# Two layer norms finished on ScalarE, two subtractions and additions moved into PSUM, and a new order of VectorE's work in a fused RWKV and FP4 kernel

## The chip, the cores and the metric

The kernel runs on one core of one Trainium2 chip. The metric is the device time of one execution in microseconds (us); lower is better. The engines are called by the profile's names: PE (TensorE, with PEld for its weight loads), DVE (VectorE), ACT (ScalarE), POOL (GpSimd) and SP (SyncE, which issues the DMAs). PSUM is the memory that PE writes; SBUF holds all else on the chip.

## What is computed

Input is x of 4 x 1024 x 256 in float32. A time-mixing block with a decaying state and a feed-forward block with block-wise quantised operands follow one another, each behind a residual and a layer norm.

```python
xx = jnp.concatenate([x[:, 1:2, :], x[:, :-1, :]], axis=1) - x
xk = x + xx * time_mix_k            # and xv, xr, xg
r = xr @ W_r.T; k = xk @ W_k.T; v = xv @ W_v.T
g = jax.nn.sigmoid(xg @ W_g.T)
state = state * w + k_t v_t^T ; out_t = state @ r_t      # scan over t, 16 heads of 16
y = attn * g @ W_o.T
y = (y - mu) / jnp.sqrt(var + EPS) * ln_gamma + ln_beta
x = _layernorm(x + y)
...
scale = jnp.max(jnp.abs(xb), axis=-1, keepdims=True) / 6.0      # blocks of 16
q = _GRID[jnp.searchsorted(_MID, jnp.abs(xb / scale))] * jnp.sign(xb) * scale
h = jax.nn.silu(q(x) @ q(w_gate).T) * (q(x) @ q(w_up).T)
x = _layernorm(x + q(h) @ q(w_down).T)
```

## The kernel before

The 4096 tokens are 32 tiles of 128 (NT = 32, 8 to a batch, TPB = 8). The work is a software pipeline: in step n every engine does its part of several tiles at once. Each engine has its own function `tiles()` whose loop runs n from 0 to 35, and the instructions of an engine run strictly in the order in which they stand there. Engines meet at semaphores (`wait_ge`, `then_inc`). Nothing but this order and the semaphores sets when something runs. A second path for fast decays exists, is chosen at run time and is not taken here.

In step n, tile n is projected (r, v, g, k) and its 16 score blocks are made; tile p = n-1 has its attention output, its gate, the projection by W_o, the norm of that (**first norm**), the residual and the **second norm** (which gives x1), and then x1 is quantised; tile m2 = n-2 has its quantised x transposed and multiplied by the gate and up weights; tile m3 = n-3 has silu, the product h, and its quantisation; tile m4 = n-4 has the down product, the residual (u2) and the **third norm**, which gives the output.

On DVE, with the names that the prediction uses:
- `late<-late,psum` (L1527) is h = silu(gate) * up of tile m3. Its start is taken as the start of a step. `hstep(m3, 0..6)` are the seven instructions that quantise h (704 columns: maximum, scale, reciprocal, L1164, L1167, L1170, L1172), `xstep(p, 0..6)` the same seven on x1 (256 columns). The seventh of h, `hstep(m3, 6)`, is followed by POOL's `scale_hidden`.
- `mix_in(n, R/V/G/K)` are the token mixes, two instructions each (L1435). `keys` (L1445) moves k to SBUF, `gate_power` (L1453) prepares the gate, `gated_out` (L1461) is `attn`.
- `statistics` (L1487), `moments` (L1494) and an addition of EPS that gives `veps` (L1561 for the first norm; L1594 for the second and third norm in one instruction of two columns) are a norm's start. POOL raises `veps` to the power -0.5, which gives `rstd` (`first_rstd` L470, `late_rstds` L476). DVE then ends the second norm in one instruction, x1 = (u - mean) * rstd (L1602), and the third in another (L1610).
- `xq_lo` (L1565): gate and up products use x in two parts, `xq_hi`, a rounded copy that ACT takes from PSUM (`high_x`), and the rest, `xq_lo` = PSUM - `xq_hi`, on DVE.
- `state_sum` (L1472), `state_half` (L1477) and `state_next` (L1482) add the tile's outer products to the state and multiply by the decay in two halves, 128 x 64 each. The last tile of a batch has none of them.

On POOL a step is `scale_x` (xq, L443), `difference(n)` (shift, L458), `add_beta` (xb, L465), `first_rstd`, `late_rstds`, `scale_hidden` (hq, L451) and four masks of 128 x 512 on the scores (L484). On ACT it is silu (L706), `copy_x` of tile n, `copy_r_v`, `high_x`, `split_r` (L678, two), `tanh_g` (L685), `copy_v`, four copies of scores (L699) and `copy_hidden`. On PE it is the transpose of x (tile n), `down`, `sums` and `outs` (L1013) of tile p, the projections with `project_out` (L872) between them, the transposes of xq and v, `gate_up_in` three times with `scores_of` and the transposes of hq between them.

The transposed x, the transposed quantised x and the transposed v share one PSUM bank (B_T); y shares a bank with the gate product (B_GATE).

The prologue quantises the feed-forward weights on DVE in seven pieces, `weights(...)`, seven instructions a piece; POOL's `dequantize` follows each. Before the change pieces 0 to 3 stand in step 0, piece 4 at the start of step 1, and pieces 5 and 6 at the end of step 2.

## Time and profile before

| | us |
|---|---|
| median of 3 runs | 661.55 (661.51 to 662.45) |
| the profiled execution | 661.79 |
| its span, first to last instruction | 660.0 |
| DVE busy | 572.3 (87%) |
| PE busy | 544.2 (82%) |
| POOL busy | 257.5 (39%) |
| ACT busy | 216.8 (33%) |
| start of step 4, of step 32 (DVE L1527) | 109.84, 612.98 |

The rows below are copied from the trace. In a timeline each row is one instruction, or a few equal ones merged (x2, x4: the time is that of all), with its start, its duration from issue to end, and in brackets the idle time of its engine before it and what released it. DVE starts an instruction that needs nothing about 0.08 us before the recorded end of the one in front. So what an instruction costs in a chain is the distance between two starts, and the recorded duration is a little longer than that.

### The profile page before, as it was taken

What the parts mean: (1) busy time and instruction counts of PE and PEld (TensorE: products, weight loads), DVE (VectorE), ACT (ScalarE), POOL (GpSimd) and SP (SyncE); (2) the same over time, 40 slices, a digit from 0 to 9 for tenths busy, and PEclk for the clock granted to TensorE, in tenths of its full rate; (3) what the DMA queues carried; (4) which work ended last, traced back from release to release, by engine and by line L of the source; (5) the groups of instructions that cost most, each with busy time, mean ns of one, the idle gap of its engine ahead of it and who ended that gap; (6) DMA issues with size and microseconds to landing.
All of it is one profiled execution on the core that took longest, in us unless ns stands there. A gap on an engine that the chain in (4) does not pass through costs nothing.

```text
span 660.0 us, 13499 instructions
## 1 busy us (share of the span) xinstructions
PE 544.2 (82%) x4928; PEld 432.8 (66%) x4928; DVE 572.3 (87%) x1445; ACT 216.8 (33%) x507; POOL 257.5 (39%) x345
## 2 busy tenths in 40 slices
PE   1557829998898988889889888988989899888754
PEld 1436628777776777767777777777767677777543
DVE  2875779999999999999999999999999999999972
ACT  1323404333333333333333333323333333333110
POOL 2152234444343334444444343334444444343311
PEclk9857959999999999999999999999999999999996
DMA  8000000000000000000000000000000000000000
GB/s 267 23 1 1 1 1 2 17 17 17 17 3 16 17 17 18 18 17 17 18 17 16 18 9 10 17 18 17 18 17 17 17 17 9 9 10 2 17 8 20
DMA packets 14041, 13.07 MB, mean 20 GB/s; under 512 B 2577, under 2 KB 13713, under 8 KB 13969
## 3 DMA queue, kind: packets, MB, share of 16 engines
q1 hardware_dynamic: 12608, 10.82, 5.4%
q10 hardware_dynamic: 1360, 1.31, 0.6%
q8 instruction: 42, 0.69, 0.5%
q14 instruction: 31, 0.25, 0.1%
HBM read 7.93 MB, written 4.19 MB: 18 GB/s over the span
## 4 chain that ended last, share of the span: by engine, by line
DVE 44%; issue 32%; POOL 10%; PE 4%; ACT 1%; POOLq 0%; DVEq 0%
DVE mix L1435 10%; POOL rstd L476 6%; DVE late L1527 4%; DVE late L1164 4%; DVE x_scale L1160 2%; DVE x_grid L1164 2%; POOL rstd L470 2%; DVE late L1167 2%; DVE x_grid L1170 2%; DVE stats L1487 2%; DVE attn L1461 2%; DVE late_down L1610 2%; DVE x_scale L1158 2%; DVE h_inv L1162 1%; DVE x_mag L1167 1%
## 5 line engine op out<-in xcount | busy, mean ns | idle before, releaser
L858 PE MATMUL psum<-mix,proj_t 128*128 128x128 f32 x768 | 111.3, 291 | 49.1 <-DVE mix L1435 47.4
L858 PEld LDWEIGHTS psum<-mix,proj_t 128*128 128x128 f32 x768 | 99.3, 198 | 66.9 <-DVE mix L1435 63.0
L665 ACT COPY rv<-psum 128x512 f32<-128x512 f32 x32 | 18.7, 585 | 238.3 <-PE psum L858 238.3
L476 POOL TENSOR_TENSOR rstd<-veps,neg_half 128x2 f32<-128x2 f32 (+1 forms) x35 | 42.2, 1205 | 129.4 <-DVE veps L1594 129.4
L978 PE MATMUL psum<-down_t,hq_t 128*128 128x256 f32 x384 | 91.2, 389 | 0.9 <-ACT hq_t L714 0.9
L1435 DVE SCALAR_TENSOR_TENSOR mix<-shift,mu,x_t 128x128 f32<-128x128 f32 x256 | 81.9, 362 | 9.0 <-POOL shift L458 5.6
L699 ACT COPY scores<-psum 128x512 f32<-128x512 f32 x128 | 65.7, 601 | 63.9 <-PE psum L1036 63.9
L470 POOL TENSOR_TENSOR rstd<-veps,neg_half 128x1 f32<-128x1 f32 x32 | 17.4, 545 | 175.8 <-DVE veps L1561 175.8
L484 POOL TENSOR_SCALAR_AFFINE_SELECT scores<-scores 128x512 f32<-128x512 f32 x128 | 81.0, 665 | 7.1 <-ACT scores L699 7.1
L978 PEld LDWEIGHTS psum<-down_t,hq_t 128*128 128x128 f32 x384 | 72.2, 195 | 10.8 <-ACT hq_t L714 2.0
L850 PE MATMUL psum<-gu_hi,xq_hi 128*128 128x512 f32 (+1 forms) x192 | 64.8, 418 | 4.5 <-DVE xq_lo L1565 4.5
L1602 DVE TENSOR_SCALAR x<-u,mv,rstd 128x256 f32<-128x256 f32 x32 | 44.8, 1401 | 15.3 <-POOL rstd L476 15.3
L850 PE MATMUL psum<-gu_lo,xq_hi 128*128 128x512 f32 (+1 forms) x192 | 56.6, 376 | 0.0
L850 PE MATMUL psum<-gu_hi,xq_lo 128*128 128x512 f32 (+1 forms) x192 | 56.2, 374 | 0.0
L886 PE MATMUL psum<-ident,hq 128*128 128x128 f32 x192 | 28.6, 286 | 19.2 <-POOL hq L451 19.2
L451 POOL TENSOR_TENSOR hq<-late,h_scale 128x704 f32<-128x704 f32 x32 | 44.3, 1384 | 0.0
L872 PE MATMUL psum<-proj_t,attn 128*128 128x256 f32 x128 | 37.6, 418 | 7.5 <-DVE attn L1461 7.5
L886 PEld LDWEIGHTS psum<-ident,hq 128*128 128x128 f32 x192 | 21.0, 143 | 32.6 <-POOL hq L451 32.5
L850 PEld LDWEIGHTS psum<-gu_hi,xq_lo 128*128 128x128 f32 x192 | 35.6, 188 | 5.8
L443 POOL TENSOR_TENSOR xq<-x_grid,x_scale 128x256 f32<-128x256 f32 x32 | 19.9, 621 | 49.8 <-DVE x_grid L1172 49.7
L850 PEld LDWEIGHTS psum<-gu_hi,xq_hi 128*128 128x128 f32 x192 | 29.0, 190 | 15.5 <-issue 9.9
L850 PEld LDWEIGHTS psum<-gu_lo,xq_hi 128*128 128x128 f32 x192 | 35.6, 188 | 5.4
(130 smaller groups left out, 1062.0 us busy)
## 6 DMA issues: line engine op xcount, KB each, us to landing
x_tok<-in_L_attn_x_dram SPq DMA_DIRECT2D x32, 128.0 KB, 2.3
out_dram<-late_down SPq DMA_DIRECT2D x32, 128.0 KB, 1.7
late_down<-in_L_ffn_w_down_dram SPq DMA_DIRECT2D x1, 704.0 KB, 6.3
late<-in_L_ffn_w_gate_dram SPq DMA_DIRECT2D x1, 640.0 KB, 6.7
late<-in_L_ffn_w_up_dram SPq DMA_DIRECT2D x1, 640.0 KB, 7.3
scores<-in_L_attn_W_r_dram ACTq DMA_DIRECT2D x1, 256.0 KB, 3.5
scores<-in_L_attn_W_v_dram ACTq DMA_DIRECT2D x1, 256.0 KB, 6.1
scores<-in_L_attn_W_g_dram ACTq DMA_DIRECT2D x1, 256.0 KB, 7.5
```

The lines of the kernel that those rows point to most:

```text
L451: g.tensor_tensor(blocks(hq[:, m % 2, 0:HID], nb), blocks(h_grid, nb), per_block(h_scale, nb), ALU.mult).then_inc(hq_ready, 1)
L476: g.tensor_tensor(rstd[:, lo:hi], veps[:, lo:hi], neg_half.broadcast_to([P, hi - lo]), ALU.pow).then_inc(late_rstd, 1)
L484: g.affine_select(out=a, in_=a, compare_op=ALU.is_ge, fill=0.0, base=0, pattern=[[0, 4], [1, P]], channel_multiplier=-1).then_inc(s_masked, 1)
L699: s.copy(scores[:, n % 2, 4 * q:4 * q + 4, :], s_bank[q].rearrange("p (h n) -> p h n", h=4)).then_inc(s_moved, 1)
L850: mm = t_.matmul(dst, x[:, slot, k], w[:, k, o:o + dst.shape[1]], start=(n == 0), stop=(n == len(parts) - 1))
L858: mm = t_.matmul(dst[:, m * P:(m + 1) * P], proj_t[:, i, k, m * P:(m + 1) * P], mix[:, slot, i, k], start=(k == 0), stop=(k == KC - 1))
L872: mm = t_.matmul(B_GATE[:, 0:C], attn[:, slot, k], proj_t[:, 4, k], start=(k == 0), stop=(k == KC - 1))
L886: mm = t_.transpose(b[:, (j % 4) * P:(j % 4 + 1) * P], hq[:, slot, j * P:(j + 1) * P], ident)
L978: mm = t_.matmul(B_S0[:, 0:C], hq_t[:, m % 2, j], down_t[:, j], start=(j == 0), stop=(j == NH - 1))
L1164: ins = v.scalar_tensor_tensor(d3, s3, -BELOW, per_block(inv[0:rows], nb), ALU.mult, ALU.mult)
L1435: ins = v.scalar_tensor_tensor(mix[:, n % 2, i, k], shift[:, n % 2, k], mu[:, i, k:k + 1], x_t[:, n % 2, k, 1:P + 1], ALU.mult, ALU.add)
L1602: v.tensor_scalar(x1[:, p % TPB], u, mv[:, 1, 0:1], rstd[:, 1:2], ALU.subtract, ALU.mult).then_inc(x1_done, 1)
```

## The change

- **Second and third norm.** DVE no longer ends them. It adds EPS separately for each (`steady`, 128 x 1), POOL takes each power separately (`second_rstd`, `third_rstd`), DVE forms nmr = -mean * rstd (`minus_mean`, 128 x 1), and ACT computes rstd * u + nmr in an Identity activation (`normalise_x`, `normalise_y`). `third_rstd` stands behind the four masks on POOL; `minus_mean(2)` stands behind the fourth instruction of `xstep` on DVE; `normalise_x` stands ahead of the four copies of scores on ACT, `normalise_y` at the end of the step, ahead of the next silu.
- **Low part of x.** PE adds -1 * `xq_hi` to the transposed x in PSUM (`take_high`, one product of a minus identity with 128 x 256), and ACT copies the difference (`low_x`). DVE's subtraction goes.
- **State.** PE adds the old state to the outer products in PSUM by eight products of 32 x 32 with the identity; DVE's `state_sum` goes and `state_half` reads PSUM.
- **Next x.** The transpose, the copy and the difference of x for tile n+1 stand at the end of step n. `scale_x(p)` stands at the end of step n instead of the start of n+1, the product with B_GATE ahead of the transposes of v.
- **Order on DVE.** The fourth instruction on h comes ahead of `gated_out`; u2's statistics come after the seventh; mix G comes ahead of the first norm's statistics; h's sixth instruction ahead of u1.
- **Prologue.** Weight pieces 0 and 1 stand ahead of the first mix, 2 in the middle of step 0, 3 at its end, piece 4 is spread over step 1, pieces 5 and 6 over step 2 (`between`). The wait for gamma and beta moves to the first use. The down weights are loaded ahead of gamma and beta.

```diff
+        minus_ident = sb("minus_ident", [P, P], F32R)
-        s_part = sb("s_part", [P, KC, 2 * D])
...
-            def late_rstds(n):
-
-                lo, hi = 1 if live(n - 1) else 2, 3 if live(n - DEEP) else 2
-                pool.wait_ge(eps_ready, n)
-                g.tensor_tensor(rstd[:, lo:hi], veps[:, lo:hi],
-                                neg_half.broadcast_to([P, hi - lo]), ALU.pow).then_inc(late_rstd, 1)
+            def second_rstd(p):
+
+                pool.wait_ge(norm2_step, N2 * p + 3)
+                g.tensor_tensor(rstd[:, 1:2], veps[:, 1:2], neg_half, ALU.pow).then_inc(x_rstd, 1)
+
+            def third_rstd(m):
+
+                pool.wait_ge(norm3_step, N3 * m + 4)
+                g.tensor_tensor(rstd[:, 2:3], veps[:, 2:3], neg_half, ALU.pow).then_inc(y_rstd, 1)
...
+                    if live(p):
+                        if p == 0:
+                            pool.wait_ge(ln_in, 16 * 2)
+                        add_beta(p)
+                        first_rstd(p)
+                        second_rstd(p)
...
-                    if n:
-                        late_rstds(n)
...
                         for i in range(QUADS):
                             mask(n, i)
-                    if n == 2:
-                        dequantize(5)
-                        dequantize(6)
-                        pad_hidden()
+                    if live(n - DEEP):
+                        third_rstd(n - DEEP)
+                    if live(n + 1):
+                        difference(n + 1)
+                    if live(p):
+                        scale_x(p)
...
+            def low_x(m):
+
+                act.wait_ge(xq_less, m + 1)
+                wait(act, gu_done, m - 1)
+                s.copy(xq_lo[:, m % 2], B_T[:, 0:C].rearrange("p (k n) -> p k n", k=KC)
+                       ).then_inc(xq_t_ready, 1)
+
+            def normalise_x(p):
+
+                act.wait_ge(norm2_step, N2 * (p + 1))
+                wait(act, norm3_step, N3 * (p - TPB) + 1)
+                normalised(x1[:, p % TPB], u, 1, x1_done)
+
+            def normalise_y(m):
+
+                act.wait_ge(norm3_step, N3 * (m + 1))
+                act.wait_ge(y_stored[m % 2], 16 * (m // 2) + 1)
+                normalised(y_out[:, m % 2], u2, 2, y_ready)
+
...
+                    if live(n - 2):
+                        low_x(n - 2)
+                    if live(n):
                         tanh_g(n)
...
                         copy_v(n)
+                    if live(n - 1):
+                        normalise_x(n - 1)
+                    if live(n):
                         for i in range(QUADS):
...
+                    if live(n + 1):
+                        copy_x(n + 1)
                     if live(n - 3):
                         copy_hidden(n - 3)
+                    if live(n - DEEP):
+                        normalise_y(n - DEEP)
...
-                wait(pe, s_added, (TPB - 1) * b + c)
+                wait(pe, s_half_ready, (TPB - 1) * b + c)
...
-                                       start=True, stop=True, skip_group_check=True)
+                                       start=(hf == 0), stop=(c == 0), skip_group_check=True)
                 mm.then_inc(u_done, 1)
                 if c:
                     pe.wait_ge(state_ready, (TPB - 1) * b + c)
+                    for hf in range(KC):
+                        for q in range(4):
+                            rows = slice(32 * q, 32 * q + 32)
+                            t_.matmul(B_O[rows, 256 + 32 * hf:256 + 32 * hf + 32],
+                                      ident[rows, rows], state[rows, c % 2, hf],
+                                      start=False, stop=True, skip_group_check=True)
...
+            def turn_quantised(m):
+
+                for k in range(KC):
+                    mm = t_.matmul(B_T[:, k * P:(k + 1) * P], xq[:, m % TPB, k * P:(k + 1) * P], ident,
+                                   is_transpose=True, start=(k == 0), stop=False,
+                                   skip_group_check=True)
+                mm.then_inc(xq_tr, 1)
+
+            def take_high(m):
+
+                pe.wait_ge(xq_copied, m + 1)
+                t_.matmul(B_T[:, 0:C], minus_ident, xq_hi[:, m % 2].rearrange("p k n -> p (k n)"),
+                          start=False, stop=True, skip_group_check=True).then_inc(xq_less, 1)
...
+            v.tensor_scalar(minus_ident, ident, -1.0, None, ALU.mult).then_inc(tab_step, 1)
...
-            def state_sum(p):
+            def state_half(p):
 
                 b, c = p // TPB, p % TPB
+                wait(dve, state_ready, (TPB - 1) * b + c)
                 part = B_O[:, 256:256 + 4 * D].rearrange("p (k n) -> p k n", k=KC)
-                if c == 0:
-                    v.tensor_copy(s_part, part).then_inc(s_added, 1)
-                else:
-                    dve.wait_ge(state_ready, (TPB - 1) * b + c)
-                    v.tensor_tensor(s_part, part, state[:, c % 2], ALU.add).then_inc(s_added, 1)
-
-            def state_half(p):
-
-                dve.wait_ge(s_added, (TPB - 1) * (p // TPB) + p % TPB + 1)
-                v.tensor_tensor(s_half, s_part, half_decay, ALU.mult).then_inc(s_half_ready, 1)
+                v.tensor_tensor(s_half, part, half_decay, ALU.mult).then_inc(s_half_ready, 1)
 
...
+            def steady(i, sem, value):
+
+                dve.wait_ge(sem, value)
+                v.tensor_scalar(veps[:, i:i + 1], mv[:, i, 1:2], EPS, None, ALU.add).then_inc(sem, 1)
+
+            def minus_mean(i, rsem, rvalue, sem):
+
+                dve.wait_ge(rsem, rvalue)
+                v.scalar_tensor_tensor(nmr[:, i:i + 1], mv[:, i, 0:1], -1.0, rstd[:, i:i + 1],
+                                       ALU.mult, ALU.mult).then_inc(sem, 1)
 
...
                         gate_power(n)
                     if live(p):
-                        moments(1, norm2_step, 2 * p + 1, drain)
-                    if n:
-                        lo, hi = 1 if live(p) else 2, 3 if live(m4) else 2
-                        need(dve, norm2_step, p + 1, 2)
-                        wait(dve, norm3_step, N3 * (m4 + 1))
-                        v.tensor_scalar(veps[:, lo:hi], mv[:, lo:hi, 1], EPS, None, ALU.add
-                                        ).then_inc(eps_ready, 1)
-                    hstep(m3, 6)
-                    moves = live(p) and p % TPB != TPB - 1
-                    if moves:
-                        state_half(p)
-                    if live(p):
-                        dve.wait_ge(late_rstd, n)
-                        v.tensor_scalar(x1[:, p % TPB], u, mv[:, 1, 0:1], rstd[:, 1:2],
-                                        ALU.subtract, ALU.mult).then_inc(x1_done, 1)
-                    if moves:
+                        minus_mean(1, x_rstd, p + 1, norm2_step)
+                    if live(m4):
+                        moments(2, norm3_step, N3 * m4 + 2, drain)
+                    if live(p) and p % TPB != TPB - 1:
                         state_next(p)
-                    xstep(p, 0)
                     if live(m4):
-                        dve.wait_ge(late_rstd, n)
-                        dve.wait_ge(y_stored[m4 % 2], 16 * (m4 // 2) + 1)
-                        v.tensor_scalar(y_out[:, m4 % 2], u2, mv[:, 2, 0:1], rstd[:, 2:3],
-                                        ALU.subtract, ALU.mult).then_inc(y_ready, 1)
-                    for k in range(1, QN):
+                        steady(2, norm3_step, N3 * m4 + 3)
+                    between(n, 5)
+                    between(n, 6)
+                    for k in range(4):
+                        xstep(p, k)
+                    if live(m4):
+                        minus_mean(2, y_rstd, m4 + 1, norm3_step)
+                    for k in range(4, QN):
                         xstep(p, k)
                     if n == 0:
                         for i in range(4):
                             low_part(i)
-                    if n == 2:
-                        weights(5, 6)
+                        weights(3)
```

DVE from the EPS addition of the second norm to the next step's L1527 (nmr is minus mean times rstd), before:

```order
L1594 TENSOR_SCALAR veps<-mv 128x2 [waits norm3_step,norm2_step]
L1172 SCALAR_TENSOR_TENSOR late<-late 128x704 [waits hquant_step]
L1477 TENSOR_TENSOR s_half<-s_part,half_decay 128x64 [waits s_added]
L1602 TENSOR_SCALAR x<-u,mv,rstd 128x256 [waits late_rstd]
L1482 TENSOR_TENSOR state<-s_half,half_decay 128x64 [waits s_half_ready]
L1158 TENSOR_REDUCE x_scale<-x 128x16 [waits xq_ready,x1_done]
L1610 TENSOR_SCALAR late_down<-late_down,mv,rstd 128x256 [waits y_stored0,late_rstd]
L1160 TENSOR_SCALAR x_scale<-x_scale 128x16 [waits xquant_step]
```

and after:

```order
L1548 TENSOR_SCALAR veps<-mv 128x1 [waits norm2_step]
L1228 SCALAR_TENSOR_TENSOR late<-late 128x704 [waits hquant_step]
L1536 BN_STATS stats<-late_down 128x6 [waits norm3_step]
L1510 SCALAR_TENSOR_TENSOR gate_pow<-sig_g,half_pow 128x256 [waits tanh_ready]
L1553 SCALAR_TENSOR_TENSOR nmr<-mv,rstd 128x1 [waits x_rstd]
L1543 BN_AGGR mv<-stats 128x2 [waits norm3_step]
L1531 TENSOR_TENSOR state<-s_half,half_decay 128x64 [waits s_half_ready]
L1548 TENSOR_SCALAR veps<-mv 128x1 [waits norm3_step]
L1214 TENSOR_REDUCE x_scale<-x 128x16 [waits xq_ready,x1_done]
L1216 TENSOR_SCALAR x_scale<-x_scale 128x16 [waits xquant_step]
L1218 RECIPROCAL x_inv<-x_scale 128x16 [waits xquant_step]
L1220 SCALAR_TENSOR_TENSOR x_grid<-x,x_inv 128x256 [waits xquant_step]
```

The second norm's end (L1602) and the third's (L1610) are gone; two small instructions on nmr stand there, the first right behind gate_pow, which moved behind the seventh instruction on h, the second inside the quantisation of x.

POOL, one step, before:

```order
L476 TENSOR_TENSOR rstd<-veps,neg_half 128x2 [waits eps_ready]
L451 TENSOR_TENSOR hq<-late,h_scale 128x704 [waits h_tr,hquant_step]
L484 AFFINE_SELECT scores<-scores 128x512 [waits s_moved] x4
L443 TENSOR_TENSOR xq<-x_grid,x_scale 128x256 [waits xq_tr,xquant_step]
L458 TENSOR_TENSOR shift<-x_t 128x256 [waits mixed,x_t_ready]
L465 TENSOR_TENSOR xb<-x_tok,beta_b 128x256 [waits norm1_step,x_in3]
L470 TENSOR_TENSOR rstd<-veps,neg_half 128x1 [waits norm1_step]
```

and after:

```order
L474 TENSOR_TENSOR rstd<-veps,neg_half 128x1 [waits norm2_step]
L450 TENSOR_TENSOR hq<-late,h_scale 128x704 [waits h_tr,hquant_step]
L486 AFFINE_SELECT scores<-scores 128x512 [waits s_moved] x4
L479 TENSOR_TENSOR rstd<-veps,neg_half 128x1 [waits norm3_step]
L457 TENSOR_TENSOR shift<-x_t 128x256 [waits mixed,x_t_ready]
L442 TENSOR_TENSOR xq<-x_grid,x_scale 128x256 [waits xq_tr,xquant_step]
L464 TENSOR_TENSOR xb<-x_tok,beta_b 128x256 [waits norm1_step,x_in2]
```

One power of two columns became two of one column, of which one stands ahead of hq and one behind the masks; shift and xq moved to the end of the step.

ACT from the copy of v on, before:

```order
L692 COPY v_tok<-psum 128x256 [waits u_done,v_tr]
L699 COPY scores<-psum 128x512 [waits o_done,s_done] x4
L712 COPY hq_t<-psum 128x512 [waits down_done,h_tr]
L714 COPY hq_t<-psum 128x256
L706 ACTIVATE late<-psum 128x704 [waits hid_step,gu_done]
L655 COPY x_t<-psum 128x2x128 [waits mixed,x_tr]
L659 COPY x_t<-x_t 128x2 [waits x_moved]
```

and after:

```order
L698 COPY v_tok<-psum 128x256 [waits u_done,v_tr]
L602 ACTIVATE x<-u,nmr,rstd 128x256 [waits norm3_step,norm2_step]
L705 COPY scores<-psum 128x512 [waits o_done,s_done] x4
L661 COPY x_t<-psum 128x2x128 [waits mixed,x_tr]
L665 COPY x_t<-x_t 128x2 [waits x_moved]
L718 COPY hq_t<-psum 128x512 [waits down_done,h_tr]
L720 COPY hq_t<-psum 128x256
L602 ACTIVATE late_down<-late_down,nmr,rstd 128x256 [waits y_stored1,norm3_step]
L712 ACTIVATE late<-psum 128x704 [waits hid_step,gu_done]
```

The second norm's activation (x) stands in front of the copies of scores and the third's (late_down) in front of silu; x_t moved ahead of hq_t.

## Rows read from the trace of the kernel before

**Rows 1.** busy us (instructions): PE, PEld, DVE, ACT, POOL; then granted clock

```profile
127.80:595.00 467.20, 420.84 (x3957) 335.75 (x3957) 434.12 (x1110) 165.90 (x390) 195.28 (x260) 1.00 0.05 15
```

**Rows 2.** timeline of DVE: start of step 4 and of step 32

```profile
109.84 0.89 DVE L1527 TENSOR_TENSOR late<-late,psum 128x704 f32<-128x704 f32 x1
...
612.98 0.88 DVE L1527 TENSOR_TENSOR late<-late,psum 128x704 f32<-128x704 f32 x1
```

**Rows 3.** timeline of DVE, one step: start us, us, instruction, [idle before, releaser]

```profile
307.49 0.88 DVE L1527 TENSOR_TENSOR late<-late,psum 128x704 f32<-128x704 f32 x1
...
313.37 0.43 DVE L1487 BATCH_NORM_STATS2 stats<-psum 128x6 f32<-128x256 f32 x1
...
315.71 0.88 DVE L1170 SCALAR_TENSOR_TENSOR late<-late 128x704 f32<-128x704 f32 x1
...
317.50 0.42 DVE L1445 TENSOR_TENSOR kd<-psum,ipow 128x256 f32<-128x256 f32 x1 [0.51 <-PE psum L865]
...
318.70 0.17 DVE L1594 TENSOR_SCALAR veps<-mv 128x2 f32<-128x2 f32 x1
318.78 0.88 DVE L1172 SCALAR_TENSOR_TENSOR late<-late 128x704 f32<-128x704 f32 x1
...
320.26 1.47 DVE L1602 TENSOR_SCALAR x<-u,mv,rstd 128x256 f32<-128x256 f32 x1 [0.46 <-POOL rstd L476]
321.65 0.65 DVE L1482 TENSOR_TENSOR state<-s_half,half_decay 128x64 f32<-128x64 f32 x1
322.23 0.41 DVE L1158 TENSOR_REDUCE x_scale<-x 128x16 f32<-128x256 f32 x1
...
322.88 0.60 DVE L1160 TENSOR_SCALAR x_scale<-x_scale 128x16 f32<-128x16 f32 x1
...
325.48 0.88 DVE L1527 TENSOR_TENSOR late<-late,psum 128x704 f32<-128x704 f32 x1
```

**Rows 4.** timeline of POOL in the same step

```profile
318.95 1.27 POOL L476 TENSOR_TENSOR rstd<-veps,neg_half 128x2 f32<-128x2 f32 x1 [3.36 <-DVE veps L1594]
320.20 1.38 POOL L451 TENSOR_TENSOR hq<-late,h_scale 128x704 f32<-128x704 f32 x1
321.53 2.50 POOL L484 TENSOR_SCALAR_AFFINE_SELECT scores<-scores 128x512 f32<-128x512 f32 x4
```

**Rows 5.** timeline of ACT in the same step

```profile
314.83 0.85 ACT L678 ACTIVATE r_par<-psum,parity 128x256 f32<-128x256 f32 x2
...
319.69 2.05 ACT L699 COPY scores<-psum 128x512 f32<-128x512 f32 x4 [2.02 <-PE psum L1036]
...
323.60 0.76 ACT L706 ACTIVATE late<-psum 128x704 f32<-128x704 f32 x1 [0.20 <-PE psum L850]
```

**Rows 6.** timeline of PE in the same step

```profile
312.02 1.13 PE L872 MATMUL psum<-proj_t,attn 128*128 128x256 f32 x4 [0.24 <-DVE attn L1461]
...
326.31 0.33 PE L992 MATMUL psum<-kd,v_tok 128*32 128x32 f32 x16
```

**Rows 7.** timelines, POOL and DVE: instructions alone, and beside one of the other engine

```profile
58.69 0.55 POOL L476 TENSOR_TENSOR rstd<-veps,neg_half 128x1 f32<-128x1 f32 x1 [3.35 <-DVE veps L1594]
...
103.69 1.13 POOL L476 TENSOR_TENSOR rstd<-veps,neg_half 128x1 f32<-128x1 f32 x1 [3.36 <-DVE veps L1594]
...
59.28 0.41 DVE L1602 TENSOR_SCALAR x<-u,mv,rstd 128x256 f32<-128x256 f32 x1 [0.54 <-POOL rstd L476]
...
35.35 0.95 DVE L1453 SCALAR_TENSOR_TENSOR gate_pow<-sig_g,half_pow 128x256 f32<-128x256 f32 x1
...
47.79 0.77 POOL L465 TENSOR_TENSOR xb<-x_tok,beta_b 128x256 f32<-128x256 f32 x1
...
47.90 0.81 DVE L1435 SCALAR_TENSOR_TENSOR mix<-shift,mu,x_t 128x128 f32<-128x128 f32 x1
```

**Rows 8.** timelines of DVE in the fourth step and of PE in the drain

```profile
92.59 1.06 DVE L1435 SCALAR_TENSOR_TENSOR mix<-shift,mu,x_t 128x128 f32<-128x128 f32 x2 [2.43 <-POOL shift L458]
...
632.03 0.73 PE L850 MATMUL psum<-gu_hi,xq_hi 128*128 128x512 f32 x2 [2.93 <-DVE xq_lo L1565]
```

136 lines of the change are left out of this document (70 added, 66 removed).

## The prediction

> **What bounds the kernel now.** I read the table of busy time by stretch first, then the timeline of one step on each engine, then looked for instructions that take longer in one place than in another. From step 4 to step 32 a step lasts (612.98 - 109.84) / 28 = 17.97 us [rows 2], so these 28 steps are 503 of the 660 us of the span, and the step decides. In the stretch of 26 steps DVE is busy 434.1 / 26 = 16.7 us a step and PE 420.8 / 26 = 16.2 [rows 1], at the full clock. DVE bounds it, PE is close behind.
>
> Inside a step I count from the start of h (L1527) as 0. DVE reaches the first norm's statistics at 5.88, the sixth instruction on h at 8.22, keys at 10.01 behind a wait of 0.51, the EPS addition of the second norm at 11.21, x1 at 12.77 behind a wait of 0.46, the maximum over x1 at 14.74, the next h at 17.99 [rows 3]. POOL raises to the power from 11.46 to 12.73, scales h (hq) until 14.09 and masks until 16.54 [rows 4].
>
> Three of these are long for what they are. x1 takes 1.47 us in the step and 0.41 elsewhere [rows 3, 7]. It starts at 12.77, 0.06 us after hq on POOL, and ends at 14.24, 0.15 after hq ends [rows 3, 4]. State takes 0.65 and x_scale 0.60 while the masks run [rows 3]. So a DVE instruction that reads or writes SBUF in a certain way stands still while a POOL instruction runs, and the other way round: the power of one column takes 0.55 alone, and 1.13 when the long L1172 has started just before it [rows 7]. In the step it takes 1.27, with L1172 started 0.17 earlier [rows 3, 4].
>
> **What the change removes on DVE.** Per step: x1, from 12.77 to 14.16 = 1.39, and the wait of 0.46 in front of it; the output's instruction, about 0.33 (322.88 - 322.23 = 0.65 for it and the maximum in front); xq_lo and the state's sum, taken like instructions of 128x256 and 128x64, 0.34 and 0.15. That is 2.7 us. It adds one more EPS addition and two nmr of one column, 0.1 each, and a few places where an instruction now directly needs the one in front, 0.1 each. Were nothing else in the way, DVE would need 15.5 to 16 us, and PE would be the bound. PE gains 8 products of 32x32, about the 0.33 of the 16 instructions of the like sums [rows 6], and one of 256 columns, 0.15 to 0.4 (below a third of the 1.13 of the four of project_out): 0.4 to 0.7, so 16.6 to 17 us. ACT has 165.9 / 26 = 6.4 us of work [rows 1] and gains four activations of 0.4 to 0.5, since two of 256 columns take 0.85 [rows 5]; its room is ample, its order is what matters.
>
> **What the change puts in a row.** I walk the new step with the durations of the rows.
>
> First half. h, its maximum, mixes R and V, scale and reciprocal, L1164's successor: as before, but u2 and its statistics no longer stand ahead, and the fourth instruction on h does: attn from 4.1 to 4.5. The projection by W_o needs it: 4.6 to 5.7, by its 1.13 [rows 6]. First statistics at 5.8 (before 5.88), mix K, EPS at 6.9, then the sixth instruction on h (0.88). POOL's first power now stands behind that one, as 1.13 stands to 0.55, and is done at 8.3; u at 8.3, its statistics at 8.8. Mix K is done at 6.7, so PE's G and K projections end at 9.0, tanh at 9.4, keys at 9.5, EPS of the second norm at 10.0. Before it was 11.2: **1.2 us gained** in this half.
>
> Second half. The seventh instruction on h starts at 10.1, so the second power is held up by it as now: it ends 1.52 after the start of the EPS addition for two columns [rows 3, 4], 0.14 earlier for one [rows 4, 7], at 11.4. hq is next on POOL at once. DVE does u2's statistics and gate_pow (until 11.7) and comes to nmr at 11.6. **Here is the step on which my forecast rests.** nmr reads two tiles in SBUF, mean and rstd, as gate_pow reads two. gate_pow took 0.95 instead of 0.41 beside a scaling on POOL [rows 7]. And which of two waiting ones goes first? A mix that was issued 0.11 after xb started on POOL, directly behind another mix, took 0.81 and ended after it, 48.71 against 48.56 [rows 7]: the one that asked first goes first. hq asks at 11.4, nmr at 11.6. So nmr ends after hq, at 12.85 (1.38 from 11.4, up to 0.2 more where gate_pow holds hq up). That it is one column wide does not save it by the rows: the power of one column was held up as well (1.13), and x_scale of 16 columns too (0.60).
>
> The Trainium skill, SBUF — State Buffer, section Who interferes with whom, says the same in general: an instruction of VectorE with two SBUF inputs contends with a GpSimd instruction that reads SBUF, and "the other fully blocks". It makes no exception for small ones, and it speaks against this change, since `minus_mean` brings such an instruction in right behind the start of hq.
>
> Then ACT's normalise_x: 12.9 to 13.35. It stands in front of the four copies of scores, whose products are done at 11.7 (now 2.2 after keys [rows 3, 5], which is at 9.5). The copies start at 13.3, last 2.05 [rows 5], and POOL's masks start after the first, at 13.95, not right after hq: 2.5 to 2.6 for four [rows 4], to 16.5. Then third_rstd, 0.55, to 17.0. DVE meanwhile has done state, the maximum over x1 at 13.4, and three more, to 14.9, and comes to `minus_mean(2)`. **This is the new wait**: it needs third_rstd, so DVE is idle from 14.9 to 17.05. Shift follows on POOL at once, reads SBUF as well and holds nmr up by another 0.4 to 0.5 (256 columns of hq's kind, about 0.6 by its 1.38 for 704), to 17.5. Three instructions of x remain, 1.1 us, to 18.65. On ACT normalise_y (17.6 to 18.0) stands in front of silu, 0.76 [rows 5], which ends at 18.8. The next h starts at **18.8 to 18.9**.
>
> The same addition made for the step before gives 17.7 to 18.2 where 17.97 is measured, by how much a held instruction delays the next. Taken at the middle, the new step is 0.9 us longer: 28 x 0.9 = +25, and +1 for the step from 3 to 4.
>
> **Prologue and drain.** Step 3 lost 2.43 us to the wait for shift [rows 8], because pieces 5 and 6 come after all of step 2 on DVE and ahead of shift on POOL. Spread over step 2 they fill waits for PE and ACT there. I take 4 us gained over the first four steps (bounds: 1 us lost, since pieces 0 and 1, eight instructions of the length of L1170, 0.8 us from start to start, and six short ones, now stand ahead of the first mix, and 7 gained). In the drain PE waited 2.93 for xq_lo [rows 8], which no longer comes behind DVE's work, and hq no longer stands behind the power of the third norm in the last step; nmr and an activation come on at the very end: 1 us gained (0 to 3).
>
> **Sum.** 660.0 + 25 + 1 - 4 - 1 = 681. The profiled execution took 1.8 more than its span, and the median is 0.2 below it: **683 us**, 3% slower. Its own range: the activation at 0.38 instead of 0.45 or at 0.6 moves the step by -0.1 or +0.3, the counting by 0.2 either way, the prologue by 5: 672 to 692.
>
> **Rivals.**
> - *nmr is not held up* (too small to need the port for any time). Speaks for it: no row shows a DVE instruction of one column with two inputs beside POOL. Then nmr is done at 11.7, normalise_x at 12.2, and the copies start with the scores. The masks follow hq as now, 12.9 to 15.4, third_rstd to 15.95, nmr of y behind shift or not to 16.5 or 16.1, the next h at 17.6 to 17.7. A gain of 0.3 x 28 = 8, with 5 of prologue and drain: 648 us, **faster**. The point from which it decides: nmr must be done by 11.9, when the scores are.
> - *PE bound.* None of the waits forms, DVE is through in 16, and the step is PE's 16.6 to 17.2: 28 x -1.0, less 5: 629 to 638 us. Against it: third_rstd behind the masks is in the order, whatever nmr does, so DVE would have to be late enough not to notice, and nothing makes it so.
> - *The waits cancel, no change*: nmr is held only for part of hq, the step is 18.1 to 18.2 and the prologue pays for it. About 660.
> - *Still slower*: an activation costs more than its kind, as by a table load each step, or PE's clock falls with its longer waits. 700 or more.
>
> **Chances.** Forecast 0.62, nmr free 0.27, PE bound 0.05, cancel 0.03, still slower 0.03. Of the forecast's 0.62 nearly all is within 672 to 692. From 646 to 692 leaves out PE bound, about a third of the free case, and the slow one: some 0.17. A measurement of this kernel tells 0.2% from no change. Faster by over 0.2%: 0.27 + 0.05 + half of cancel = 0.33; within: 0.02; slower: 0.65.
>
> **What the profile after would show.** L1553, the first of a step, at about 1.3 us and ending 0.1 to 0.2 after hq; if it takes 0.15, the first rival holds. Copies of scores 1.5 us or more after the scores' products, released by the activation. DVE idle some 2 us in front of the second L1553, released by POOL's L479. The EPS of the second norm at 10.0 after L1595; steps of 18.9. Step 4 starting 2 to 4 us earlier than 109.84. I am wrong if nmr's own time is short, if the masks start with hq's end, or if the wait for L479 is absent.

## The result and the profile after

The changed kernel takes 682.04 us (median of 4 runs, 681.0 to 682.85) against 662.0 us (661.51 to 663.15) for the kernel before: a ratio of 1.0299, with a 95% interval of 1.0279 to 1.032. It is 3% slower. Its profiled execution took 681.0 us with a span of 678.9.

First the starts of step 4 and of step 32 on DVE, which answer [rows 2]: start us, us, engine, line, operation, [idle before, releaser].

```profile
97.34 0.89 DVE L1595 TENSOR_TENSOR late<-late,psum 128x704 f32<-128x704 f32 x1 [0.24 <-ACT late L712]
...
632.83 0.89 DVE L1595 TENSOR_TENSOR late<-late,psum 128x704 f32<-128x704 f32 x1 [0.19 <-ACT late L712]
```

A step lasts (632.83 - 97.34) / 28 = 19.12 us, against 17.97. The 18.9 us by which the span grew are three terms: step 4 starts 12.5 us **earlier** (97.34 against 109.84), the 28 steps take 32.35 us **more** (535.49 against 503.14), and from the start of step 32 to the end it is 46.1 us against 47.0, so 0.95 less.

The busy time of a stretch of 26 steps, which answers [rows 1] (us from the start, length; busy us and instructions of PE, PEld, DVE, ACT, POOL; granted clock, DMA share, GB/s):

```profile
116.78:614.09 497.31, 432.87 (x4352) 345.29 (x4351) 408.25 (x1087) 199.23 (x468) 227.55 (x287) 1.00 0.05 15
```

DVE is busy for 15.7 us of a step (before 16.7), PE for 16.65 (before 16.2), both at the full clock. So a step of 19.12 is longer than any engine's busy time: it has waits in it that no one engine's work explains. The timeline of one step shows which. Its start is h at 308.07. DVE, which answers [rows 3]:

```profile
308.07 0.89 DVE L1595 TENSOR_TENSOR late<-late,psum 128x704 f32<-128x704 f32 x1 [0.19 <-ACT late L712]
...
318.15 0.15 DVE L1548 TENSOR_SCALAR veps<-mv 128x1 f32<-128x1 f32 x1
...
319.36 0.41 DVE L1510 SCALAR_TENSOR_TENSOR gate_pow<-sig_g,half_pow 128x256 f32<-128x256 f32 x1
319.68 1.35 DVE L1553 SCALAR_TENSOR_TENSOR nmr<-mv,rstd 128x1 f32<-128x1 f32 x1
...
321.70 0.42 DVE L1214 TENSOR_REDUCE x_scale<-x 128x16 f32<-128x256 f32 x1 [0.39 <-ACT x L602]
...
325.35 0.56 DVE L1553 SCALAR_TENSOR_TENSOR nmr<-mv,rstd 128x1 f32<-128x1 f32 x1 [2.22 <-POOL rstd L479]
...
327.22 0.89 DVE L1595 TENSOR_TENSOR late<-late,psum 128x704 f32<-128x704 f32 x1 [0.19 <-ACT late L712]
```

POOL in the same step, which answers [rows 4]:

```profile
318.38 1.12 POOL L474 TENSOR_TENSOR rstd<-veps,neg_half 128x1 f32<-128x1 f32 x1 [2.00 <-DVE veps L1548]
319.48 1.54 POOL L450 TENSOR_TENSOR hq<-late,h_scale 128x704 f32<-128x704 f32 x1
322.21 2.59 POOL L486 TENSOR_SCALAR_AFFINE_SELECT scores<-scores 128x512 f32<-128x512 f32 x4 [1.20 <-ACT scores L705]
324.77 0.55 POOL L479 TENSOR_TENSOR rstd<-veps,neg_half 128x1 f32<-128x1 f32 x1
325.28 0.61 POOL L457 TENSOR_TENSOR shift<-x_t 128x256 f32<-128x256 f32 x1
```

ACT, which answers [rows 5]:

```profile
321.07 0.60 ACT L602 ACTIVATE x<-u,nmr,rstd 128x256 f32<-128x256 f32 x1 [1.96 <-DVE nmr L1553]
321.57 2.03 ACT L705 COPY scores<-psum 128x512 f32<-128x512 f32 x4
...
325.94 0.60 ACT L602 ACTIVATE late_down<-late_down,nmr,rstd 128x256 f32<-128x256 f32 x1 [1.08 <-DVE nmr L1553]
326.45 0.74 ACT L712 ACTIVATE late<-psum 128x704 f32<-128x704 f32 x1
```

Read together they are one chain. nmr, one column wide, is issued at 319.68 and ends at 321.03, 0.01 after hq (319.48 + 1.54). Of the 64 uses of L1553 in the whole execution, 30 take 1.33 to 1.35 us, 27 take 0.56 and 7, at the start and in the drain, 0.15 or 0.16. ACT has waited 1.96 us for it; only then come the activation, the copies of scores, and on POOL the masks, which left POOL idle for 1.20. The third power comes behind the masks; DVE has been idle for 2.22 when it is done. The second nmr ends at 325.91, 0.02 after shift; then the third norm's activation, silu, and the next h.

### The profile page after: what moved, and what is told of

It is laid out like the page before. It is cut to its first block, busy times and chain, and to the rows that moved or that the text cites. A ratio compares the mean times of both kernels' runs of the same rounds, so it can differ in the third digit from the quotient of the medians.

```text
span 678.9 us, 14607 instructions
## 1 busy us (share of the span) xinstructions
PE 556.1 (82%) x5408; PEld 443.7 (65%) x5408; DVE 542.6 (80%) x1415; ACT 258.0 (38%) x603; POOL 292.2 (43%) x374
## 4 chain that ended last, share of the span: by engine, by line
DVE 37%; PE 21%; issue 17%; POOL 14%; ACT 9%; ACTq 1%; DVEq 0%; POOLq 0%
PE psum L893 10%; POOL scores L486 9%; DVE nmr L1553 8%; DVE mix L1492 6%; PE psum L907 5%; DVE late L1595 4%; PE psum L900 4%; DVE late L1228 4%; ACT late L712 3%; ACT scores L705 3%; POOL rstd L479 2%; DVE kd L1502 2%; DVE attn L1518 2%; ACT sig_g L691 2%; DVE stats L1536 2%
## 5 line engine op out<-in xcount | busy, mean ns | idle before, releaser
L469 POOL TENSOR_TENSOR rstd<-veps,neg_half 128x1 f32<-128x1 f32 x32 | 35.1, 1096 | 187.7 <-DVE veps L1548 187.7
L1553 DVE SCALAR_TENSOR_TENSOR nmr<-mv,rstd 128x1 f32<-128x1 f32 x64 | 56.7, 886 | 65.6 <-POOL rstd L479 65.3
L671 ACT COPY rv<-psum 128x512 f32<-128x512 f32 x32 | 18.8, 586 | 226.6 <-PE psum L893 226.6
L1013 PE MATMUL psum<-down_t,hq_t 128*128 128x256 f32 x384 | 94.1, 396 | 8.9 <-ACT hq_t L720 8.9
L486 POOL TENSOR_SCALAR_AFFINE_SELECT scores<-scores 128x512 f32<-128x512 f32 x128 | 83.3, 684 | 34.7 <-ACT scores L705 34.6
L1492 DVE SCALAR_TENSOR_TENSOR mix<-shift,mu,x_t 128x128 f32<-128x128 f32 x256 | 80.4, 357 | 4.5 <-POOL shift L457 4.5
L885 PE MATMUL psum<-gu_hi,xq_hi 128*128 128x512 f32 (+1 forms) x192 | 68.5, 438 | 1.5 <-DVE u L1632 1.1
L474 POOL TENSOR_TENSOR rstd<-veps,neg_half 128x1 f32<-128x1 f32 x32 | 35.3, 1103 | 65.6 <-DVE veps L1548 65.6
L450 POOL TENSOR_TENSOR hq<-late,h_scale 128x704 f32<-128x704 f32 x32 | 48.4, 1513 | 14.2 <-DVE late L1228 14.2
L1054 PE MATMUL psum<-scores,kd 128*32 128x128 f32 x1024 | 36.3, 285 | 12.1 <-POOL scores L486 12.1
L602 ACT ACTIVATE x<-u,nmr,rstd 128x256 f32<-128x256 f32 x32 | 19.2, 600 | 62.8 <-DVE nmr L1553 62.8
L885 PEld LDWEIGHTS psum<-gu_hi,xq_hi 128*128 128x128 f32 x192 | 31.7, 192 | 13.7 <-issue 9.9
```

The lines of the kernel that those rows point to most:

```text
L450: g.tensor_tensor(blocks(hq[:, m % 2, 0:HID], nb), blocks(h_grid, nb), per_block(h_scale, nb), ALU.mult).then_inc(hq_ready, 1)
L474: g.tensor_tensor(rstd[:, 1:2], veps[:, 1:2], neg_half, ALU.pow).then_inc(x_rstd, 1)
L486: g.affine_select(out=a, in_=a, compare_op=ALU.is_ge, fill=0.0, base=0, pattern=[[0, 4], [1, P]], channel_multiplier=-1).then_inc(s_masked, 1)
L885: mm = t_.matmul(dst, x[:, slot, k], w[:, k, o:o + dst.shape[1]], start=(n == 0), stop=(n == len(parts) - 1))
L1013: mm = t_.matmul(B_S0[:, 0:C], hq_t[:, m % 2, j], down_t[:, j], start=(j == 0), stop=(j == NH - 1))
L1054: mm = t_.matmul(B_O[32 * q:32 * q + 32, hf * P:(hf + 1) * P], kd[:, p % 4, 32 * h:32 * h + 32], scores[:, p % 2, 4 * q + i], start=(p % T ...
```

## The experiments

Times are medians, in each group beside runs of the kernel before on the same chip: 661.83 us (7 runs) for e1 to e4, 661.61 (13 runs) for e5, e6, e8 and e10, 662.11 (19 runs) for e9 and e11 to e13. Ratios are to these, with the 95% interval. The theory is the prediction's: nmr is held up by hq, and the order behind it turns that into the longer step. The rival is that the hold-up is only seen there, and that ScalarE's slower activation, the new order or the added work of PE would make the step long anyway.

### e1: nmr as an instruction with one tensor input

```
-                v.scalar_tensor_tensor(nmr[:, i:i + 1], mv[:, i, 0:1], -1.0, rstd[:, i:i + 1],
-                                       ALU.mult, ALU.mult).then_inc(sem, 1)
+                v.tensor_scalar(nmr[:, i:i + 1], mv[:, i, 0:1], rstd[:, i:i + 1], -1.0,
+                                ALU.mult, ALU.mult).then_inc(sem, 1)
```

> The changed kernel, with both nmr written as an instruction of one tensor input: mean times rstd times -1, where rstd is a per-partition scalar instead of a second tensor. Same result, same place, same waits. Theory A (the first nmr is held up because it reads two tiles in SBUF beside POOL's hq): its duration falls from 1.35 to about 0.15 us, the second's from 0.56 to 0.15, the activation behind it and the copies of scores start with the scores' products, the step of 19.12 us becomes 17.6 to 17.9, the time 682 becomes 640 to 648. Theory B (the nmr is long because any small DVE instruction stands still beside hq, or because DVE's queue is late there): nothing changes, 680 to 684. Theory C (only the power behind the masks costs time): the first nmr gets short but the step stays within 0.3 us, 674 or more.

Measured: 639.43 us, 0.6 below the range expected, ratio 0.9658 (0.9639 to 0.9677), steps of 17.64 us. DVE, POOL and ACT at the place of the rows above:

```profile
304.18 0.20 DVE L1553 TENSOR_SCALAR nmr<-mv,rstd 128x1 f32<-128x1 f32 x1
...
304.39 1.20 DVE L1531 TENSOR_TENSOR state<-s_half,half_decay 128x64 f32<-128x64 f32 x1
...
308.70 0.21 DVE L1553 TENSOR_SCALAR nmr<-mv,rstd 128x1 f32<-128x1 f32 x1 [1.64 <-POOL rstd L479]
```

```profile
303.97 1.54 POOL L450 TENSOR_TENSOR hq<-late,h_scale 128x704 f32<-128x704 f32 x1
305.56 2.59 POOL L486 TENSOR_SCALAR_AFFINE_SELECT scores<-scores 128x512 f32<-128x512 f32 x4
```

```profile
304.42 0.60 ACT L602 ACTIVATE x<-u,nmr,rstd 128x256 f32<-128x256 f32 x1 [0.82 <-DVE nmr L1553]
```

The same product, beside the same hq, takes 0.20 instead of 1.35 (all 64 uses of L1553 take 0.20 to 0.22), and 42.6 us are gone, more than twice what the whole change lost. The hold-up itself is not gone: state, the next instruction with two tensors in SBUF, now takes 1.20 and ends at 305.59, 0.08 after hq. But no other engine waits for state there, and DVE, which does, is idle for 1.64 a little later anyway, while ACT's activation and, behind it, the copies of scores and the masks waited for nmr. The masks now start right behind hq. This settles the step on which the forecast rested, and its rival in the other direction (nmr free) is the kernel measured here.

### e2 and e3: the third power ahead of the masks

```
                     if live(n - 3):
                         scale_hidden(n - 3)
+                    if live(n - DEEP):
+                        third_rstd(n - DEEP)
                     if live(n):
                         for i in range(QUADS):
                             mask(n, i)
-                    if live(n - DEEP):
-                        third_rstd(n - DEEP)
```

> The changed kernel, with POOL's power of the third norm ahead of the four masks instead of behind them. The first nmr is still held by hq. Theory A: the wait of 2.22 us in front of the second nmr goes, the masks start as late as before, and the step is 18.0 to 18.3 instead of 19.12: 651 to 660. Theory B, its rival: the masks set the step (copies, masks, attention output), so that the power's place only moves the wait to PE's attention output or to the mixes: 676 or more.

e3 is this edit and that of e1.

> Both edits at once: nmr with one tensor input, and the power of the third norm ahead of the masks. Theory A says that then nothing of DVE, POOL or ACT stands in front of PE: the step is PE's, 16.8 to 17.3 us, the time 620 to 632, below both kernels. If the two waits were one and the same (rival), both edits together give no more than the better of the two alone, about 645.

Measured: e2 649.99 us, ratio 0.982 (0.9795 to 0.9846), steps of 17.94; e3 615.93 us, ratio 0.9304 (0.9285 to 0.9324), steps of 16.80. Each is a little better than the range expected of it. In e2 nmr is still held (1.35) and the second nmr finds its power done; 1.18 us a step came from that wait alone. e3, one step on DVE:

```profile
282.56 0.89 DVE L1595 TENSOR_TENSOR late<-late,psum 128x704 f32<-128x704 f32 x1
...
294.16 0.21 DVE L1553 TENSOR_SCALAR nmr<-mv,rstd 128x1 f32<-128x1 f32 x1
...
294.38 1.20 DVE L1531 TENSOR_TENSOR state<-s_half,half_decay 128x64 f32<-128x64 f32 x1
...
297.07 0.20 DVE L1553 TENSOR_SCALAR nmr<-mv,rstd 128x1 f32<-128x1 f32 x1
297.19 0.59 DVE L1223 TENSOR_SCALAR x_mag<-x_grid 128x256 int32<-128x256 int32 x1
297.82 0.73 DVE L1226 SCALAR_TENSOR_TENSOR x_grid<-x_mag,x_grid 128x256 f32<-128x256 f32 x1
...
299.38 0.89 DVE L1595 TENSOR_TENSOR late<-late,psum 128x704 f32<-128x704 f32 x1
```

PE and ACT at the end of the same step:

```profile
298.25 2.86 PE L1013 MATMUL psum<-down_t,hq_t 128*128 128x256 f32 x12 [0.29 <-ACT hq_t L720]
```

```profile
298.59 0.76 ACT L712 ACTIVATE late<-psum 128x704 f32<-128x704 f32 x1
```

The only idle time of DVE left between the two h is 0.18 in front of keys. But DVE alone doesn't bound this step. PE's only idle time in it is the 0.29 above, and silu ends at 299.35, 0.03 before h, at the end of a row of ACT's work that runs without a pause from the first nmr on. The last step of a batch is without `state_next`, which takes DVE 1.12 from start to start in the others, and yet it lasts 16.71 instead of 16.82: h there waits 0.32 for silu. So DVE, PE and ACT are full together, and the expectation, which had the step as PE's, named only one of them. DVE's share is stretched by POOL: besides state, x_mag takes 0.59 and x_grid 0.73 beside the masks, where the changed kernel, with the masks over by then, has 0.28 and 0.42. e3 is 7% faster than the kernel before and the best of all that ran: the change with two lines mended.

### e8 and e9: the two norms ended on VectorE again

Everything else of the change stays. At the places of the two nmr DVE ends the norms as it did before, x1 and the output each in one instruction; the two activations are gone.

```
-                        minus_mean(1, x_rstd, p + 1, norm2_step)
+                        dve.wait_ge(x_rstd, p + 1)
+                        v.tensor_scalar(x1[:, p % TPB], u, mv[:, 1, 0:1], rstd[:, 1:2],
+                                        ALU.subtract, ALU.mult).then_inc(x1_done, 1)
...
-                    if live(n - 1):
-                        normalise_x(n - 1)
```

> The changed kernel, with the two norms ended on DVE again in one instruction each (as in before), at the places where the two instructions on nmr stand; the two activations and nmr are gone, all else is as changed. It measures what ScalarE's part of the norms costs or gives. Theory A (the activation in front of the copies of scores is what makes nmr's hold-up expensive): x1 is held until hq ends, at about 12.9 to 13.1 of the step, but the copies of scores start with the scores at 11.9, the masks right behind hq, the third power at 15.9, and the next h at 17.6 to 17.9: 28 steps of 17.7, 640 to 646 us. Theory B (the added work of DVE, 0.65 us a step, and the same waits cost as much as ScalarE's part did): steps of 18.7 to 19.2, 670 to 685 us. I expect A.

Measured: 645.23 us, ratio 0.9767 (0.9744 to 0.979), steps of 17.83. DVE, POOL and ACT of one step:

```profile
306.70 1.49 DVE L1654 TENSOR_SCALAR x<-u,mv,rstd 128x256 f32<-128x256 f32 x1
...
311.19 0.69 DVE L1669 TENSOR_SCALAR late_down<-late_down,mv,rstd 128x256 f32<-128x256 f32 x1 [1.05 <-POOL rstd L479]
```

```profile
306.50 1.54 POOL L450 TENSOR_TENSOR hq<-late,h_scale 128x704 f32<-128x704 f32 x1
307.99 2.64 POOL L486 TENSOR_SCALAR_AFFINE_SELECT scores<-scores 128x512 f32<-128x512 f32 x4
```

```profile
306.81 2.06 ACT L705 COPY scores<-psum 128x512 f32<-128x512 f32 x4 [0.68 <-PE psum L1073]
```

x1 is held as nmr was (1.49, until 0.15 after hq), and it costs nothing on POOL: the copies of scores no longer stand behind it, and the masks follow hq at once. So the changed kernel splits in two: all of the change but ScalarE's norms takes the kernel from 661.6 to 645.2, and ScalarE's norms, as made, add 36.8.

e9 adds the move of the third power to that.

> The kernel with the norms ended on VectorE again, and the third power on POOL also put ahead of the four masks. Norms on VectorE alone gave steps of 17.81 us and 645.2 us, with 1.05 us of idle time in front of the third norm. The pair without these norms (one-input nmr and the power first) gave 16.80 a step and 615.9 us. If ScalarE's norms are a gain once no wait hangs on them: VectorE does 0.6 us a step more here and its step is 16.9 to 17.4, 618 to 634 us, 5 to 15 above that pair. If TensorE bounds both: 16.8 and 615 to 617. I expect 17.1 and 625.

Measured: 638.57 us, ratio 0.9648 (0.9619 to 0.9677), steps of 17.64. That is 13.6 us above the value expected and 4.6 above its range. Between two h of a step DVE is idle only for 0.18 in front of keys, and silu is done 1.6 before h, so DVE bounds this kernel. Since it is idle as little in e3, the two steps differ by its work: against e3, x1 costs 1.40 from start to start where nmr costs 0.12 (1.28 more), state is not held behind it (0.11 instead of 1.12), and the output costs 0.64 instead of 0.12 (0.5 more). Together 0.8, which is 17.6 less 16.8. I had counted 0.6, by their durations alone, and not that the third norm's instruction would be stretched by the masks (0.72); the rest of the miss is that 17.1 was set below 16.80 + 0.6. So ScalarE's norms are a gain of 0.8 us a step where no engine waits behind them, and a loss of 1.3 (19.12 less 17.83) in the place where the change put them.

### e11: the one-input form, two columns wide

```
-                v.scalar_tensor_tensor(nmr[:, i:i + 1], mv[:, i, 0:1], -1.0, rstd[:, i:i + 1],
-                                       ALU.mult, ALU.mult).then_inc(sem, 1)
+                v.tensor_scalar(nmr[:, 2 * i:2 * i + 2], mv[:, i, 0:2], rstd[:, i:i + 1], -1.0,
+                                ALU.mult, ALU.mult).then_inc(sem, 1)
```

> The changed kernel with nmr by the one-input instruction (which alone gave 639.4 us and 0.20 us beside hq), but two columns wide: it multiplies mean and variance by rstd and -1, and only the first result is used. All else as changed. It changes one size, and asks what frees the instruction. VectorE's x1, 256 columns of the same one-input instruction with two per-partition scalars, is held by hq (1.49 us) in the kernel with the norms on VectorE, so the number of tensor inputs does not settle it alone. Theory A (a single column is what frees the one-input form): with two columns nmr takes 1.3 to 1.4 us and ends after hq, and the time is 680 to 684. Theory B (what is held is long or wide; two columns are as free as one): 0.2 us, 639 to 641.

Measured: 683.56 us, ratio 1.0339 (1.0297 to 1.0381), steps of 19.15. DVE and POOL:

```profile
322.09 1.36 DVE L1553 TENSOR_SCALAR nmr<-mv,rstd 128x2 f32<-128x2 f32 x1
...
327.77 0.57 DVE L1553 TENSOR_SCALAR nmr<-mv,rstd 128x2 f32<-128x2 f32 x1 [2.22 <-POOL rstd L479]
```

```profile
321.89 1.53 POOL L450 TENSOR_TENSOR hq<-late,h_scale 128x704 f32<-128x704 f32 x1
```

With one column more the whole loss is back: theory A. Neither the number of tensor inputs nor the length alone decides. With two tensors in SBUF one column is held (1.35 in the changed kernel); with one tensor in SBUF one column is free (0.20) and two columns are held (1.36), as x1 with 256 is (1.49).

The Trainium skill names both ways of being held. SBUF — State Buffer, section Who interferes with whom, has two SBUF inputs contending with a GpSimd instruction that reads SBUF, and also the faster mode that takes both pairs of ports; VectorE: DVE Perf Modes, section What auto-detection actually checks, says that this mode is taken with one source and the destination in SBUF where the outermost dimensions that are not 1 are both even or equal. The traces agree for one column with two inputs (1.35) and for 2 and 256 columns with one (1.36, 1.49). These sections don't say what holds for a single column with one input; here it is not held (0.20).

### e4, e5 and e10: the start

PE's transpose of the first tile of x waits for its DMA. Before, it stands ahead of the product that decides on the path; on DVE the tables stand behind that product. Rows of the kernel before, then of the changed one:

```profile
10.17 0.66 PE L766 MATMUL psum<-ident,x_tok 128*128 128x128 f32 x2 [10.17 <-DMA x_tok<-in_L_attn_x_dram]
...
10.99 0.15 DVE L1180 TENSOR_REDUCE idle<-psum 1x1 f32<-1x2 f32 x1 [5.41 <-PE psum L773]
...
18.88 2.19 DVE L1435 SCALAR_TENSOR_TENSOR mix<-shift,mu,x_t 128x128 f32<-128x128 f32 x8 [3.43 <-issue]
```

```profile
5.93 0.15 DVE L1236 TENSOR_REDUCE idle<-psum 1x1 f32<-1x2 f32 x1 [0.30 <-PE psum L805]
...
13.92 1.28 DVE L1214 TENSOR_REDUCE q_scale<-late 128x48 f32<-128x768 f32 x2 [3.40 <-issue]
```

e4 is the changed kernel with the transpose (and ACT's copy of it) back where it stood; e5 is the kernel before with them moved as the change does. PE's part of e5's edit:

```
             pe.wait_ge(const_step, 6)
-            transpose_x(Tile(0, 0))
             pe.wait_ge(exceeds_ready, 1)
...
             mm.then_inc(block_mm, 1)
+            transpose_x(Tile(0, 0))
```

> The changed kernel, with the transpose and the copy of the first x back ahead of the tables on PE and ACT, as before the change. Step 4 of the changed kernel starts 12.5 us earlier than before, where 3 were forecast. Theory A: 4 to 5 us of that are this move alone, since before it the sum that decides the path, and with it all of DVE's tables, stood behind a transpose that waited for x to land at 10.2 us: 686 to 687 here. Rival: the gain is the weights spread over the steps, and DVE's start is hidden: 682, unchanged.

> The kernel before, with the PE transpose of the first tile of x and its two ACT copies put behind the tables of the decays, as the changed kernel has them, and nothing else. In the trace of before the tables on DVE start at 10.99 us because PE's transpose waits for x until 10.17; beta's DMA is issued at 9.5 and lands after 5.1, at 14.6, and POOL and DVE wait for it ahead of the loop. Account A (the transposes hold the tables, and the 4.9 us go straight through): DVE's first mix at 14.0 instead of 18.88, step 4 starts 4 to 5 us earlier than 109.84, 657 us. Account B (beta's landing takes over): the loops start at 15 to 16.2, the first mix at 16.5 to 17, step 4 2 us earlier, 660 us. Account C (the tables' place did nothing, later waits absorb it): step 4 at 109 to 110, 661.8 us. I expect B.

e10 is e5 with the waits for gamma and beta moved too:

```
             pool.wait_ge(zeroed, 2)
-            pool.wait_ge(ln_in, 16 * 2)
...
                     if live(p):
+                        if p == 0:
+                            pool.wait_ge(ln_in, 16 * 2)
                         add_beta(p)
```

> The same edit of the kernel before, and the waits for gamma and beta moved from ahead of the loops on POOL and DVE to their first use, as the changed kernel has them. If these two edits are the start's part of the gain: first mix at 14.0, step 4 starts 4.5 to 5 us earlier than in before (105), 657 us. If the transposes or the weights of the projections, loaded by ACT's DMAs, take over, step 4 is less than 3 us earlier and the time is 659 or more. A step in the middle stays at 17.97 by both.

Measured: e4 688.04 us, ratio 1.0395 (1.0375 to 1.0416), step 4 at 102.21, so 4.87 later than in the changed kernel; the time is 1 us above the range expected, and from step 32 to the end this profile has 48.3 us where the changed kernel's has 46.1, which the edit doesn't explain. e5 659.27 us, ratio 0.9966 (0.995 to 0.9981), step 4 at 107.49, 2.35 earlier than before. e10 656.85 us, ratio 0.9932 (0.9913 to 0.9952), step 4 at 105.20, 4.64 earlier. The first mix of e5 and of e10:

```profile
16.43 2.19 DVE L1435 SCALAR_TENSOR_TENSOR mix<-shift,mu,x_t 128x128 f32<-128x128 f32 x8 [6.08 <-POOL shift L458]
```

```profile
14.02 2.19 DVE L1437 SCALAR_TENSOR_TENSOR mix<-shift,mu,x_t 128x128 f32<-128x128 f32 x8 [3.56 <-POOL shift L458]
```

In e5 shift starts only at 15.79, with DVE's tables done at 10.4. The trace names no releaser for it, but its account B, the wait for beta, is borne out by e10: with that wait moved too the 4.9 us go through. These kernels' steps stay at 17.97. The beginning accounts for 4.6 of the 12.5 us.

### e6: the weights in blocks again

In the changed kernel, `between` does nothing, piece 4 is quantised at the start of step 1 and pieces 5 and 6 at the end of step 2; POOL's part of 5 and 6 comes behind the masks of step 2:

```
+                    if n == 1:
+                        weights(4)
...
+                    if n == 2:
+                        weights(5, 6)
```

> The changed kernel, with the quantisation of pieces 4, 5 and 6 of the feed-forward weights put back where before has it: piece 4 in a block at the start of step 1, pieces 5 and 6 in a block at the end of step 2, POOL's part of piece 4 ahead of xb in step 1 and of 5 and 6 behind the masks of step 2, ahead of shift. Step 4 starts 12.5 us earlier in the changed kernel (97.34) than in before (109.84), of which the start of the loops accounts for 4.9. If spreading the pieces gives the rest: step 4 at 104 to 106, 689 to 691 us, and a wait of the mixes for POOL's shift in step 3. If the pieces' place is worth what the prediction took (2 us or less), step 4 at 98 to 99.5 and 683 to 684. I expect 688. A step in the middle stays at 19.12.

Measured: 689.85 us, ratio 1.0452 (1.0417 to 1.0487); step 4 at 106.21, 8.87 later than in the changed kernel; steps of 19.12. DVE in the fourth step, which answers [rows 8]:

```profile
87.97 1.42 DVE L1492 SCALAR_TENSOR_TENSOR mix<-shift,mu,x_t 128x128 f32<-128x128 f32 x2 [1.86 <-POOL shift L457]
```

The wait that was 2.43 us before is back with 1.86. Spreading the pieces is worth 8.9 us here, the larger part of what the start gave. 4.6 and 8.9 make 13.5, 1.0 more than the 12.5 found; that the two parts don't quite add up is left open.

### e12 and e13: two attempts to go further

e12 is e3 with `mix_in(n, R)` ahead of h on DVE, and `copy_hidden` ahead of `copy_x` on ACT; e13 also puts silu ahead of `normalise_y`.

```
+                    if live(n):
+                        mix_in(n, R)
                     if live(m3):
                         dve.wait_ge(sig_ready, m3 + 1)
```

> The changed kernel with the one-input nmr and the third power ahead of the masks (together 615.9 us, 16.80 a step), and two moves more: the two mixes of R on VectorE go ahead of h, where VectorE is idle for 0.32 us until silu is done, and ScalarE copies the transposed hq ahead of the transposed x, since TensorE is idle for 0.29 us until the former is there. If these two waits and the order round them bound the step: 16.3 to 16.6, 601 to 610 us. If VectorE or TensorE are at their own bound (masks on POOL stretch four of VectorE's instructions): 16.8, 615 to 617. I expect 608.

> The same with one move more: ScalarE does silu ahead of the activation that ends the third norm, which takes 0.50 us from start to start and stands in front of silu in the changed kernel. If silu is still what VectorE's h waits for: 0.1 to 0.4 us a step less than without this move, 3 to 11 us. If not: no difference over 1 us.

Measured: 659.6 us, ratio 0.9964 (0.9948 to 0.998), and 658.32 us, ratio 0.9949 (0.9936 to 0.9963); steps of 18.22 and 18.21. The expectation of e12 was wrong by 51.6 us. DVE, POOL and ACT of e12:

```profile
301.56 1.43 DVE L1492 SCALAR_TENSOR_TENSOR mix<-shift,mu,x_t 128x128 f32<-128x128 f32 x2 [0.51 <-POOL shift L457]
302.91 0.88 DVE L1597 TENSOR_TENSOR late<-late,psum 128x704 f32<-128x704 f32 x1
```

```profile
297.95 2.83 POOL L486 TENSOR_SCALAR_AFFINE_SELECT scores<-scores 128x512 f32<-128x512 f32 x4
300.74 0.78 POOL L457 TENSOR_TENSOR shift<-x_t 128x256 f32<-128x256 f32 x1
301.48 0.62 POOL L442 TENSOR_TENSOR xq<-x_grid,x_scale 128x256 f32<-128x256 f32 x1
302.06 0.77 POOL L464 TENSOR_TENSOR xb<-x_tok,beta_b 128x256 f32<-128x256 f32 x1
```

```profile
300.44 0.74 ACT L712 ACTIVATE late<-psum 128x704 f32<-128x704 f32 x1
```

The mixes need shift, which comes behind the masks and ends at 301.52; xq and xb are queued right behind it on POOL and hold the two mixes up (1.43 instead of 0.60). silu is done at 301.18, so h could have started there and starts at 302.91. I had taken the idle time in front of h (0.32) from a step at the end of a batch, which is without `state_next`; in the others DVE had none, and the mixes' own condition I had not looked up. ACT's two copies were exchanged in the same run, so their part is not separated; the waits above are the mixes'. With h so late, silu earlier by an activation (e13) gives nothing, which its steps show; the 1.3 us between the two medians lie outside the 28 steps.

## Why the prediction was right, and for what reasons

The forecast was 683 us; 682.04 was measured. Its central step is shown: one line of code, the form of nmr (e1), decides between 17.64 and 19.12 us a step. But the total is closer than its terms are, and that part is luck.

- **First half of the step.** The second norm's EPS was put at 10.0 after h, 1.2 earlier than before. It is at 318.15 - 308.07 = 10.08. Right.
- **nmr held by hq.** Put at 11.6 to 12.85, measured 11.61 to 12.96. The 0.1 is hq, which takes 1.54 instead of the 1.38 of [rows 4], within the 0.2 allowed for gate_pow.
- **Copies, masks, third power.** Copies put at 13.3, measured 13.50; masks 13.95, measured 14.14; power done at 17.0, measured 17.25. Half of the 0.2 at the copies is hq, 0.05 is the activation, the rest rounding and the masks.
- **The activation.** Taken at 0.45 (bounds 0.38 to 0.6), from PSUM activations of 256 columns [rows 5]. It takes 0.60, but what counts in the chain is the 0.50 from start to start: 0.05 more than was taken for the first, 0.1 more for the second (put at 17.6 to 18.0, measured 17.87 to 18.38).
- **The second nmr.** Put behind shift, at 17.5; it ends at 17.84, 0.34 later, of which 0.25 come from the power in front and the rest from shift, which holds it to its end (0.56 instead of the 0.4 to 0.5 taken).
- **The step.** 18.8 to 18.9 by the forecast, 19.15 in the step shown, 19.12 in the mean: 28 x 1.15 = +32.3 us instead of +25. No single term makes the 0.3 by which the chain is longer: hq has 0.1 of it, the two activations 0.15, shift's hold on the second nmr 0.1, and small gaps taken too long give a little back.
- **Busy times.** DVE 15.5 to 16 and PE 16.6 to 17 were expected and 15.7 and 16.65 came out. For DVE that is partly luck: the forecast was for a step in which nothing is held, and the 15.7 holds some 1.6 of the two nmr being held (1.35 and 0.56 against 0.15 each). ACT was said to gain four activations a step; it is three (18 instructions a step instead of 15).
- **The prologue.** This term failed. The forecast had 4 us gained (bounds 1 lost to 7 gained) and 1 lost again from step 3 to step 4, together 3; step 4 starts 12.5 earlier, and from step 3 to step 4 it is not 1 longer but 1.9 shorter (19.58 against 21.49). The step left out is the beginning of the program: I read the prologue from step 0 on, and never asked what DVE waited for at 10.99. e4, e5 and e10 show that the transpose of x and the waits for gamma and beta were worth 4.6 to 4.9; e6 shows that spreading the pieces was worth 8.9, where I had taken the one wait of 2.43 in [rows 8] and little more. The blocks also keep PE and ACT waiting, which the forecast named and didn't price.
- **The drain.** 1 us gained was forecast, 0.95 was measured. One profile of each doesn't show this term: e6 and e4, whose edits don't touch the drain, have 46.0 and 48.3 from step 32 to the end.
- **The rivals.** nmr free was given steps of 17.6 to 17.7 and 648 us; e1, which is that case, has 17.64 and 639.4: the difference is again the start. The case of a step near PE's bound (629 to 638 us) was held to be out of reach since the third power stands behind the masks; e3, which moves it, has steps of 16.80 and 615.9.

So two errors, 7.3 us too little on the steps and 9.5 too little gained at the start, offset each other to 2 in the span (681 forecast, 678.9 measured), by luck. The median comes nearer still, since it lies 1.0 above the profiled execution, where 0.2 below was taken.

## What to carry to other kernels

When an instruction is made shorter or moved to a third engine, look at what stands beside it in time: a one-column product took 1.35 us because POOL was reading SBUF, and it cost 42.6 us of 682 because the next engine's whole queue waited for it. While POOL reads, the next instruction of a kind that can be held will be; let it be one for whose result no other engine waits (state, held for 1.20 in e1 at no cost that shows), and give the one that others wait for a form that isn't held. And read the first 20 us of the trace as closely as the steady step: here they and the first three steps held 12.5 us.

## What the runs showed of the hardware that was not expected

- One column more makes the one-input instruction wait for POOL: 0.20 us with one column and 1.36 with two, beside the same hq (e1, e11). With two tensor inputs even one column waits: 1.35. Where POOL is free that form takes 0.15 to 0.16, as in the start and the drain of the changed kernel:

```profile
51.58 0.16 DVE L1553 SCALAR_TENSOR_TENSOR nmr<-mv,rstd 128x1 f32<-128x1 f32 x1
...
645.86 0.15 DVE L1553 SCALAR_TENSOR_TENSOR nmr<-mv,rstd 128x1 f32<-128x1 f32 x1
```

- ACT's activation of 256 columns from SBUF with a scale and a bias takes 0.60 us, its copy of 256 columns from PSUM 0.37 to 0.41 in the same step. Whether the source or the two operands of one column make the difference was not tried.
